# A bias product moved and more placeholders in the lead-in, and one value product behind each step's scores in the attention heads

## The reference, cut to what matters

```
def attention(x, ...):                    # on _gn(x), GroupNorm in 32 groups
    xh = x.reshape(b_, 8, 16, n)          # 8 heads of 16 channels
    q, k, v = proj(Wq, bq, xh), proj(Wk, bk, xh), proj(Wv, bv, xh)   # per head
    attn = softmax(einsum('bgdi,bgdj->bgij', q, k) * 16**-0.5)
    out = einsum('bgij,bgdj->bgdi', attn, v)
    return proj(Wp, bp, out)
def convnext(x, ...):                     # on _gn(x)
    y = depthwise 7x7 convolution(x, conv_w) + conv_b
    y = layernorm over channels (y) * ln_g + ln_b
    h = gelu(einsum('bhwc,cf->bhwf', y, w1) + b1)      # 128 -> 512
    return einsum('bhwf,fc->bhwc', h, w2) + b2
x = x + attention(_gn(x))
x = x + convnext(_gn(x))
```

## Time and profile before

| | us |
|---|---|
| median of 3 timed runs | 314.36 (313.17 to 314.5) |
| the profiled execution | 311.52 |
| its span | 309.6 |
| PE busy | 293.9 (95%) |
| DVE busy | 228.6 (74%) |
| ACT busy | 176.6 (57%) |
| POOL busy | 79.4 (26%) |

### The profile page before, as it was taken

How to read it: one execution, slowest core, us unless ns; L and a number is a source line. 1 busy time by engine, 2 the same in 40 slices (tenths; PEclk the granted TensorE clock), 3 DMA queues, 4 the chain that set the end, 5 groups by cost and what they waited for, 6 DMA issues and landing times.

```text
span 309.6 us, 5462 instructions
## 1 busy us (share of the span) xinstructions
PE 293.9 (95%) x2101; PEld 134.6 (43%) x2103; DVE 228.6 (74%) x264; ACT 176.6 (57%) x354; POOL 79.4 (26%) x103
## 2 busy tenths in 40 slices
PE   7899999999999999999999999999999989999895
PEld 2535434445445444444345445444333444323342
DVE  2858444887997988989668898998997158986321
ACT  1442134887887877877768877776318645011321
POOL 7102405233200000000002878998320100101010
PEclk9998556999999999999999999999999999999999
DMA  6275000320330330231211429800000005730001
GB/s 221 35 142 94 11 0 0 55 50 6 51 54 4 50 57 10 45 52 20 34 29 26 110 66 193 179 6 1 3 0 2 0 2 135 176 121 0 0 34 34
DMA packets 8488, 16.30 MB, mean 53 GB/s; under 512 B 2564, under 2 KB 3716, under 8 KB 8464
## 3 DMA queue, kind: packets, MB, share of 16 engines
q1 hardware_dynamic: 8048, 15.29, 23.1%
q10 hardware_dynamic: 416, 0.69, 1.0%
HBM read 4.96 MB, written 1.73 MB: 22 GB/s over the span
## 4 chain that ended last, share of the span: by engine, by line
PE 78%; DVE 9%; ACT 7%; issue 2%; DMA 1%; POOL 1%; SPq 0%; DVEq 0%; ACTq 0%; POOLq 0%
PE ps L1051 20%; PE ps L1062 19%; PE ps L1152 10%; PE ps L1004 8%; ACT pr L656 7%; DVE mx L767 5%; PE ps L1210 5%; PE ps L1224 5%; PE ps L978 2%; PE ps L1041 2%; DVE ot L777 2%; PE ps L945 1%; DMA w<-wpack 1%; PE ps L1196 1%; PE ps L1168 1%
## 5 line engine op out<-in xcount | busy, mean ns | idle before, releaser
L767 DVE TENSOR_REDUCE mx<-ps 128x1 f32<-128x1024 f32 x128 | 151.1, 1220 | 39.4 <-PE ps L1004 39.4
L656 ACT ACTIVATE pr<-ps 128x512 f32<-128x512 f32 x256 | 133.3, 603 | 53.3 <-PE ps L1051 52.8
L1051 PE MATMUL ps<-qs,ks 50*128 50x512 f32 x256 | 98.1, 451 | 6.0 <-ACT pr L656 3.6
L1004 PE MATMUL ps<-ks,qs 48*128 48x512 f32 x256 | 102.2, 464 | 1.0 <-DVE mx L767 1.0
L1051 PEld LDWEIGHTS ps<-qs,ks 50*128 50x128 f32 x256 | 43.9, 189 | 60.5 <-ACT pr L656 39.8
L1062 PE MATMUL ps<-pr,va 128*32 128x256 f32 x1024 | 69.6, 389 | 0.4 <-ACT pr L656 0.4
L1004 PEld LDWEIGHTS ps<-ks,qs 48*128 48x128 f32 x256 | 44.8, 194 | 11.7 <-DVE mx L767 4.3
L1062 PEld LDWEIGHTS ps<-pr,va 128*32 128x32 f32 x1024 | 26.8, 110 | 29.9 <-ACT pr L656 11.8
L483 POOL CAST mparts<-mx 128x8 fp32r<-128x8 f32 x16 | 3.0, 190 | 134.3 <-DVE mx L767 134.3
L805 DVE SCALAR_TENSOR_TENSOR hl<-xpad,w,hl 128x512 f32<-128x512 f32 (+1 forms) x37 | 35.6, 962 | 0.9
L1152 PE MATMUL ps<-xr,wt 128*32 128x512 f32 x272 | 31.0, 594 | 0.0
(11 more groups left out here) (104 smaller groups left out, 204.9 us busy)
## 6 DMA issues: line engine op xcount, KB each, us to landing
qs<-hl SPq DMA_DIRECT2D x48, 64.0 KB, 2.4
ks<-hl SPq DMA_DIRECT2D x47, 64.0 KB, 2.4
xr<-xpad SPq DMA_DIRECT2D x16, 95.0 KB, 2.2
xr<-pad_dram SPq DMA_DIRECT2D x4, 361.0 KB, 5.9
xr<-pad_dram SPq DMA_DIRECT2D x4, 304.0 KB, 4.8
xr<-xpad SPq DMA_DIRECT2D x8, 76.0 KB, 2.1
xr<-xpad ACTq DMA_DIRECT2D x8, 76.0 KB, 2.2
xs<-x SPq DMA_DIRECT2D x2, 256.0 KB, 2.9
```

What stands on the lines that cost most here:

```text
L656: nc.scalar.activation(pr[:, n % PR, c * HALF:(c + 1) * HALF], bank("half", n, c), ACT.Exp, scale=SCALE).then_inc(exp_done, 1)
L767: nc.vector.tensor_reduce(mx[:, s % 2, i:i + 1], sm[(NT * s + i) % 2], AX.X, ALU.max).then_inc(max_done, 1)
L1004: last = nc.tensor.matmul(sm[k % 2][:, c * HALF:(c + 1) * HALF], qs[rows, cell_of(s) + i * P:cell_of(s) + (i + 1) * P], ks[rows, cell_of(s ...
L1051: nc.tensor.matmul(bank("half", n, c), ks[rows, cell_of(t) + j * P:cell_of(t) + (j + 1) * P], qs[rows, cell_of(t) + c * HALF:cell_of(t) + ...
```

## The change

The bias product moves out of the lead-in to a place ahead of the value bias, and the addition that uses it (`b1s`) to a place ahead of the maxima; the second image's q projection waits for that addition. W1's transfer is queued behind the constants, with a semaphore of its own, and W2 gets its own too. In the lead-in the placeholders go from 9 to 15, in steps 0 and 1 of head 0 from three to two each, and ahead of the lead-in from four to three. In the heads `times_v(n - 2)` stands behind the scores of every step n, where at even steps two stood, and ACT's `copy_u` comes a step later. Cut to its core:

```
@@ block.sync @@
             sp.dma_start(bv[:, :], bvrow.rearrange("a p -> p a")).then_inc(S("bv"), 16)
+            sp.dma_start(w1s[:, :], w1).then_inc(S("w1"), 16)
...
-            sp.dma_start(w1s[:, :], w1).then_inc(S("w12"), 16)
-            sp.dma_start(w2s[:, :, :], w2.rearrange("(f p) c -> p f c", p=P)).then_inc(S("w12"), 16)
+            sp.dma_start(w2s[:, :, :], w2.rearrange("(f p) c -> p f c", p=P)).then_inc(S("w2"), 16)
@@ block.scalar, head @@
-                    if j == 0 and t:
+                    if j == LATER - 1 and t:
                         copy_u(t - 1)
@@ block.vector @@
+            v.wait_ge(S("lnb"), 1)
+            nc.vector.tensor_tensor(b1s[:, :], lnb, vec(V_B1, FC), ALU.add).then_inc(S("b1"), 1)
...
             for k in range(AHEAD):
                 maxima(*divmod(k, NT))
-                if k == 6:
-                    v.wait_ge(S("lnb"), 1)
-                    nc.vector.tensor_tensor(b1s[:, :], lnb, vec(V_B1, FC), ALU.add).then_inc(S("b1"), 1)
@@ block.tensor @@
             def first_bias():
-                t_.wait_ge(S("w12"), 32)
+                t_.wait_ge(S("w1"), 16)
+                t_.wait_ge(S("gn_ve"), B)
...
             project_v(0, 0, NT)
+            first_bias()
             value_bias()
+            t_.wait_ge(S("b1"), 1)
             project(1, 0)
@@ block.tensor, head @@
-                    if n < 2:
-                        keep_busy(3)
+                    if n < LATER:
+                        keep_busy(2)
...
-                    if j % 2 == 0 and n:
-                        times_v(n - 2)
-                        times_v(n - 1)
+                    if n >= LATER:
+                        times_v(n - LATER)
@@ block.tensor, the lead-in @@
-            keep_busy(4, sm[0][:, 0:HALF])
+            keep_busy(3, sm[0][:, 0:HALF])
             for k in range(AHEAD):
...
+                if k == 2:
+                    keep_busy(1, st[1])
...
-                if k == 5:
-                    first_bias()
...
-                if k in (4, 6, 8, 10, 11, 12):
-                    keep_busy(1 + k // 10)
+                if k >= 4 and k not in (7, 9):
+                    keep_busy(2)
```

More of the change, by code:

```diff
@@ L503, in _ @@
                 ALU.mult).then_inc(S("wt"), 1)
-            g.wait_ge(S("w12"), 32)
+            g.wait_ge(S("w1"), 16)
             nc.gpsimd.tensor_scalar(w1g[:, :], w1s[:, :], vec(V_G), 0.0, ALU.mult, ALU.add).then_inc(S("w1g"), 1)
@@ L1128, in _ @@
                 if k == 9:
-                    t_.wait_ge(S("b1"), 1)
                     turn_max(0)
-                if k in (4, 6, 8, 10, 11, 12):
-                    keep_busy(1 + k // 10)
+                if k >= 4 and k not in (7, 9):
+                    keep_busy(2)
             t_.wait_ge(S("kones"), 32)
@@ L1218, in mlp_down @@
                 if f == 0:
+                    t_.wait_ge(S("w2"), 16)
                     if k:
```

## The result

The changed kernel takes 298.25 us (median of four executions, 298.04 to 298.55), the kernel before 314.43 beside it: the ratio is 0.949, with an interval of 0.945 to 0.952. The profiled execution went from 311.52 to 298.37, 13.15 less. One thing must be known to read this: executions of the kernel before come with and without the sag of the clock, and by their times (313.17 to 315.43) those four all had it. Against executions of before at full clock the changed kernel stands at 0.991 (0.990 to 0.993). So the change does two things: it makes a full-clock execution 3 us shorter, and it makes rare a sag that costs 10 to 16 us where it comes (one of nine executions has one, and 31 of 44 before). The second is the larger.

The account below looks back on a forecast made before the run. PE's stream bounds the kernel (78% of the chain of waits), with a clock sag early on. Gains 9.4 + 3.6 + 0.3 = 13.3 us: 311.5 to 298.2 profiled, 301 at the median; 8-in-10 range 293 to 313.

Parts of the forecast that it names:

- Bias product ahead: Before the lead-in: the moved product delays the first scores from 18.16 to 19.05, a loss of 0.9 us.
- Lead-in: Row-maximum tiles before head 0: 17.7 us at full clock, so head 0 starts at 36.7 instead of 39.92.
- First steps: Head 0 up to step 5: 7.7 us, step 5 at 44.4 instead of 53.76, a gain of 9.4 us so far.
- Heads: One value product per step: two heads take 22.13 us for 22.67, a gain of 3.6 us over 13.5 heads.
- Tail: Heads 14 and 15: DVE's convolution sum sets the centring product's start; a gain of 0.3 us.
- Rival B: Ahead of the lead-in: the clock falls sooner, at about 18, giving about 320 us; chance 0.10.
- Rival C: Lead-in: the fall has a cause fillers do not reach, the clock drops at 28 as now, 312 us; chance 0.06.
- Rival A: Heads: clock stays full but tiling switches cost 3 to 10 us; 304 to 314, say 307; chance 0.13.
- Rival D: Heads: clock stays full and a lone value product costs no more than half a pair; 294 us; chance 0.04.
- the one on the median: Whole kernel: timed median lies 2.84 us above the profiled execution, carried over to turn 298.2 into 301.1.

Follow-up runs that it names:

- e2: The changed kernel with value products in pairs at even steps and the copy where it was, lead-in as changed; 302.57 us, full clock in all four executions.
- e6: The changed kernel with the row-maximum scores 16 tiles ahead instead of 13; 291.78 us, full clock in all six executions.
- e9: The changed kernel with row-maximum scores 16 tiles ahead instead of 13 and value products in pairs; 298.68 us, full clock in all four executions.
- e1: The kernel before with one value product behind each step and the copy a step later, lead-in as before; median 312.05 us, 297.42 in its one full-clock execution.
- e3: The changed kernel with the bias product back behind lead-in tile 5 and its addition behind the seventh maximum; 298.2, 298.4, 317.7 and 361.74 us.
- e8: The changed kernel with the bias product back behind lead-in tile 5 and value products in pairs; four executions at 301.9 to 303.3 us, six at 313.4 to 315.5.
- e4: The changed kernel with the 9 lead-in placeholders of before in their old places; 305.30 to 318.83 us in four executions, none at full clock.

## Why the prediction was right, and where it was not

The sum was made for the profiled execution: 311.5 - 13.3 = 298.2, measured 298.37. By its terms:

- *Bias product ahead*: the projection was to start at 16.5 and did at 16.46; the first scores at 19.05, and 19.00. A loss of 0.8 for the 0.9 of the sum. The earlier transfer of W1 cost nothing: PE reached the product at 14.95 without a wait.
- *Lead-in*: 17.7 us by the sum, 16.9 by the rows (19.00 to 35.87). Mis-sized were the halves of the value projection, 1.08 (28.14 to 29.22) and 1.00 in place of 1.2 each, the first two tiles, 1.12 together (19.00 to 20.12) in place of 1.32, and the 0.4 for waits for a maximum: there were none, and where PE waited 0.27 before (21.34) the new placeholder behind tile 2 now stands.
- *First steps*: 7.7 us; 43.59 - 35.87 = 7.72. These three terms together gave 10.2, not 9.4.
- *Heads*: two heads 22.13, and 22.13 measured. Over the 13.5 heads it should have been 3.6; the kernel before and e2 against the changed kernel both give 2.8. Up to the transposition in head 11 (180.47 before, 166.86 now) the gain is 3.4, and from there to head 14's step 3 0.6 is lost again. There DVE's divisions take 1.54 to 1.72 us beside POOL for the usual 0.29, and PE waits for maxima at the end of heads 11, 12 and 13 (0.34, 0.37, 0.53, where before it was 0.16, 0.40, 0.18). The sum, made from heads 2 and 3, left that out.
- *Tail*: 0.3 by the sum; by e2, -0.3 up to the centring product and 0.5 behind it. That DVE's sum sets the start of that product isn't borne out: in both traces PE's stream has no gap there (before, scores at 237.90 and the product at 238.56), and the two engines end level.

The terms as measured add up to 10.2 + 2.8 - 0.3 + 0.5 = 13.2. So the hit within 0.2 us is in part luck: 0.8 too little ahead of step 5 and 0.8 too much in the heads cancel.

Rival B (a fall at the bias product's new place) did not show in any of 22 executions with the bias product and the placeholders as changed (e2, e6, e9 and the changed kernel, leaving out the one whose sag is not placed). Rival C fell with them too: with both pieces 22 of 23 executions are at full clock, 13 of 44 before, so what PE runs in the lead-in (or when it runs it, which no run separates) does bear on the clock. Its premise, that PE is without a pause throughout the sag, is not quite so: PE stands still for 0.34 before 35.12. Rival A fell by the rows, two heads in 22.13; its range also doesn't follow from its words, since heads that lose 3 to 10 give 308 to 315. Rival D fell too: the lone value product costs 0.57 (45.49 to 46.06), not 0.50.

The step that failed, though the range holds the result, is the one on the median. I carried over the 2.84 by which the timed runs of before lay above its profiled execution, and so came to 301 where 298.25 was measured. That difference was no fixed cost: it was the sag, which had a mean clock of 0.961 in the profiled execution and 0.951 in later ones of 314.4; from these clocks I estimate 24 and 31 us at the lower level. A change that removes the sag removes it too. The deeper fault was to take the sag for a property of the kernel. One trace can't show how often a thing happens; three timed runs spread over 1.3 us, where full-clock ones of the changed kernel spread over 0.5, were a hint that I didn't use. That every execution of before that I had then showed the sag was chance as well: of the 39 that came after these and the result, 13 did not. Of the 16.2 us between the medians, about 4.2 come from the heads, the new lead-in takes back about 1 at full clock, and 13 are the sag (314.4 against 301.3 in the executions of before). The first is shown by e2 and its trace, with one full-clock execution of e1 beside it; the last by the executions of before themselves.

What decides whether a given execution of before sags is open: it is the same program each time.

## What to carry to other kernels

Where the granted clock sags in a profile, run the kernel a dozen times and sort the times by that clock before crediting a change with the difference; a kernel can be 1% better at full clock and 5% better in its median. Here one-column products and sparse placeholders stood before the fall in the lead-in, and neither move alone kept the clock up in every execution; with both it stayed up in 22 of 23. And where two streams of half-height products alternate, look at which row groups meet in each step: here one constant, the distance between the streams, was worth more than the whole rearrangement at full clock.

## What the runs showed of the hardware

- One and the same program had a full clock in 13 of 44 executions (301.0 to 302.0 us) and a sag in 31 (311.5 to 317.3); times with a sag cluster by their mean clock: 0.956 with some 313, 0.951 with 314.5, 0.939 with 317.1. One execution of e3 ran at half clock for some two fifths of 360 us.
- The clock fell while PE's record was without a gap (28.00 to 29.00 before, 26.00 to 28.00 in e8) as well as within 3.3 us after a gap of 0.56 (e4), and it stayed full behind the same gap in e6 (189.93): in these traces PE's busy time did not foretell a fall.
- Score products in two row groups start together and follow each other after 0.34 at most; in one row group each takes its 0.235. A lone value product costs 0.57, two in a row 1.00.
- DVE's division of 128 x 128 elements took 0.29 us with POOL quiet, and 1.54 to 1.75 where one of POOL's additions of two 128 x 1024 tensors (L570) ran beside it from its start.
